# ScalarE's small copies and gate exponentials two turns further on, in the expert stage of a decoder layer

## The reference

```python
logits = jnp.einsum('btd,ed->bte', x, gate_w)
_, idx = jax.lax.top_k(logits + lb_bias, K)               # K = 2 of E = 8
w = jax.nn.sigmoid(sel_logits); w = w / (w.sum(-1) + 1e-6)
hidden = jnp.square(jax.nn.relu(jnp.einsum('nd,ehd->neh', xf, w1)))
expert_out = jnp.einsum('neh,edh->ned', hidden, w2)
moe_out = jnp.einsum('ned,ne->nd', expert_out, we)        # we: weight of each token and expert, mostly 0
shared = jnp.square(jax.nn.relu(x @ cfc.T)) @ cproj.T
```

## Time and profile before

| | us |
|---|---|
| median of 3 runs | 491.29 (489.8 to 491.65) |
| profiled execution | 488.51 |
| its span in the trace | 486.7 |
| PE busy in the span | 440.3 (90%) |
| DVE busy | 333.7 (69%) |
| ACT busy | 265.6 (55%) |
| POOL busy | 162.1 (33%) |
| expert stage, first up to last residual add | 409.5 to 484.0 |

### The profile page before, as it was taken

The page is one execution under the profiler, slowest core; times in us unless marked ns, Lnnn a source line. Parts: engine busy times, 40 slices in busy tenths (PEclk is TensorE's granted clock), DMA queues, the critical chain, the costliest instruction groups (busy, mean ns, idle before and its releaser), DMA issues.

```text
span 486.7 us, 17235 instructions
## 1 busy us (share of the span) xinstructions
PE 440.3 (90%) x7304; PEld 276.1 (57%) x7304; DVE 333.7 (69%) x668; ACT 265.6 (55%) x811; POOL 162.1 (33%) x95
## 2 busy tenths in 40 slices
PE   0778999999999799999799999998888989999996
PEld 0444655665755555655575675574445435666765
DVE  5555787666977667886847987867677596565633
ACT  2545646666466456555535655545544456554653
POOL 7148384332350963350851432093300000001000
PEclk9999999999999899999889999999989899999999
DMA  8221000000000000000000000000000004404150
GB/s 286 70 73 48 20 9 23 26 18 9 27 25 1 24 18 11 25 24 2 24 4 24 2 5 1 3 4 2 1 1 1 1 1 174 175 23 162 35 195 24
DMA packets 17465, 19.49 MB, mean 40 GB/s; under 512 B 1659, under 2 KB 14575, under 8 KB 17263
## 3 DMA queue, kind: packets, MB, share of 16 engines
q1 hardware_dynamic: 17391, 18.41, 11.2%
HBM read 16.17 MB, written 2.16 MB: 38 GB/s over the span
## 4 chain that ended last, share of the span: by engine, by line
PE 67%; DVE 18%; issue 5%; ACT 5%; DMA 3%; POOL 1%; SPq 0%; DVEq 0%; ACTq 0%; POOLq 0%
PE psT L1489 15%; PE psS L1460 13%; PE psS L1470 8%; PE psOM L1426 7%; PE psT L1859 5%; PE psS L1842 4%; DVE neg_max L1086 2%; DVE x_max L1069 2%; ACT prob L692 2%; PE psOM L1570 2%; PE psS L1689 2%; DMA q_both<-w_scratch 2%; PE psT L1570 2%; DVE pt_even L1050 2%; PE psOM L1716 1%
## 5 line engine op out<-in xcount | busy, mean ns | idle before, releaser
L692 ACT ACTIVATE prob<-psS,neg_max 128x208 f32<-128x208 f32 (+23 forms) x256 | 120.9, 479 | 71.2 <-DVE neg_max L1086 40.1
L475 POOL TENSOR_TENSOR stat<-stat,pack_a_sb 128x4 f32<-128x4 f32 (+2 forms) x16 | 54.7, 3417 | 163.3 <-DVE stat L912 116.9
L1086 DVE TENSOR_REDUCE neg_max<-psS 128x2 f32<-128x672 f32 (+9 forms) x96 | 77.0, 802 | 43.1 <-PE psS L1470 42.3
L1489 PE MATMUL psT<-pack_a_sb,prob 128*128 128x128 f32 (+4 forms) x640 | 95.9, 285 | 6.6 <-DVE pt_even L1050 3.5
L1489 PEld LDWEIGHTS psT<-pack_a_sb,prob 128*128 128x128 f32 (+4 forms) x640 | 65.7, 133 | 45.8 <-issue 27.0
L1460 PE MATMUL psS<-k_v,q_both 64*32 64x336 f32 (+23 forms) x2048 | 88.8, 402 | 3.0 <-ACT prob L692 1.7
L1470 PE MATMUL psS<-rel_shifted,q_both 36*32 36x268 f32 (+16 forms) x2048 | 72.4, 339 | 0.0
L509 POOL TENSOR_TENSOR q_both<-qT,pack_a_sb 128x1024 f32<-128x1024 f32 x16 | 31.7, 1981 | 84.3 <-PE psS L1470 81.9
L1470 PEld LDWEIGHTS psS<-rel_shifted,q_both 36*32 36x32 f32 x2048 | 37.9, 109 | 24.5 <-issue 17.5
L692 ACT ACTIVATION_READ_ACCUMULATOR prob<-psS,neg_max 128x1 f32 x256 | 50.9, 199 | 0.0
L1859 PEld LDWEIGHTS psT<-pack_b_sb,prob 128*128 128x128 f32 x288 | 36.1, 191 | 18.3 <-DVE prob L1332 11.1
(11 more groups left out here) (173 smaller groups left out, 606.7 us busy)
## 6 DMA issues: line engine op xcount, KB each, us to landing
q_rep<-q_scratch SPq DMA_DIRECT2D x128, 32.0 KB
k_v<-w_scratch SPq DMA_DIRECT2D x8, 512.0 KB, 6.6
q_both<-w_scratch SPq DMA_DIRECT2D x8, 512.0 KB, 6.6
pack_b_sb<-pack_b_dram SPq DMA_DIRECT2D x1, 1641.5 KB, 9.7
X<-x_dram SPq DMA_DIRECT2D x4, 256.0 KB, 5.3
q_scratch<-qT SPq DMA_DIRECT2D x4, 256.0 KB, 2.0
out_dram<-X SPq DMA_DIRECT2D x4, 256.0 KB, 2.3
pack_a_sb<-pack_a_dram SPq DMA_DIRECT2D x1, 535.0 KB, 4.4
```

The lines of the kernel that those rows point to most:

```text
L475: nc.gpsimd.tensor_tensor(st[:, 5, 0:groups], st[:, 2, 0:groups], ca["root"][0:parts, 0:groups], ALU.pow).then_inc(seeded, 1)
L692: ins = nc.scalar.activation(prob[:, s % 4, half, 0:wide], psS[:, bank + half, at:at + wide], ACT.Exp, bias=neg_max[:, s % 4, half:half + ...
L1086: v.tensor_reduce(neg_max[:, s % 4], psS[:, bank:bank + 2, 0:read_width(*divmod(s, BS))], AX_X, ALU.max, negate=True).then_inc(max_ready, 1)
L1489: ins = nc.tensor.transpose(psT[0:w, k % 2, at:at + T], prob[:, s % 4, half, j * T:j * T + w], ident)
```

## The change

In the expert stage, each of ScalarE's eight small instructions stands two turns further on: behind square(k+2) where it stood behind square(k). What they compute, and the orders of TensorE, VectorE, GpSimd and SyncE, stay.

```diff
-                if b == 0 and i == 1:
+                if b == 0 and i == 3:
                     copy_weights(1, psO[0:TB * E, 0:T])
-                if b == 0 and i == 3:
+                if b == 0 and i == 5:
                     copy_back(B - 1)
-                if b == 0 and i == 4:
+                if b == 0 and i == 6:
                     copy_front(2, psO[:])
-                if b == 0 and i == 6:
+                if b == 0 and i == 8:
                     exp_gate(2, psO[:, 0:TB * E])
-                if b == 1 and i == 4:
+                if b == 1 and i == 6:
                     copy_weights(2, psM[0:TB * E, T:2 * T])
-                if b == 1 and i == 8:
+                if b == 2 and i == 1:
                     copy_front(3, psO[:])
-                if b == 2 and i == 0:
+                if b == 2 and i == 2:
                     exp_gate(3, psM[:, 0:TB * E])
-                if b == 2 and i == 6:
+                if b == 2 and i == 8:
                     copy_weights(3, psM[0:TB * E, T:2 * T])
```

## The result

| | before | after |
|---|---|---|
| median of 11 runs each (us) | 490.22 | 487.82 |
| ratio of the runs, 95% interval | | 0.9943 (0.9923 to 0.9964) |
| profiled execution | 488.51 | 487.04 |
| first up in its trace | 409.52 | 411.24 |
| expert stage, first up to the end of the last residual add | 74.45 | 71.27 |

The account below looks back on a forecast made before the run. PE, busy 90% of the span, was taken as the bound, with eight downs late behind DVE and ACT. Removed 4.21 less 0.6 added gives 3.6 us: 491.29 to 487.7 us, range 486.0 to 490.5 (8 in 10).

Parts of the forecast that it names:

- seven late downs: Downs of turns 2, 4, 7, 14, 16, 19 and 25, late before; forecast to give back 4.21 us in all.
- The rule by which a late down costs its printed idle time plus 0.27 us: PE in the expert stage: the loss per late down is about printed idle plus 0.27; 5.18 us over eight downs.
- Turn 2: Late down(2): weigh(2), freed from square(2), starts about 0.55 earlier, first weight load still not hidden; 0.55 of 0.67 us goes.
- Turn 16: Late down(16), at the end of a layer-norm chain begun after the late weigh(14): its whole 0.71 us goes.
- turn 10: Late down(10), which hangs on DVE's routing arithmetic behind e_add(0): stays late at 0.85 us.
- The tight places: Readers of moved results; tightest is gate(3) waiting for copy_front(3), 0.35 us to spare: costs nothing, at worst 0.3.
- the load behind copy_weights(3): Load that weigh(28) needs lands late, so down(28) stalls anew: 0.5 to 1.1 us, taken as 0.6.
- U + 2.1: U is the start of the up in PE's turn k; ACT reaches the moved small instruction 2.1 us later.
- The page on transfers: Advice against the change, borne out at weigh(28) alone; taken alone, the change would cost 0.6 us there and nothing else.
- Half comes back: Rival, chance 0.19: turn 16 stays late, copy_front(3) misses by 0.3, first load takes 4.4 or more; 2.1 us gained, 489.2.
- The stalls did not change their name: Rival, chance 0.10: DVE's own order would hold the weighs back instead of ACT; 0 to 1 us goes, 491 us.
- ACT kept its lead: Rival "slower", chance 0.06: square(k) comes in turn k-1 instead of k-2, each turn loses 0.4; 494.5 us for 17 turns.

Follow-up runs that it names:

- e1: Kernel before with only copy_weights(1), copy_back, copy_front(2) and exp_gate(2) moved two turns on: expert stage 72.75 us, against 74.45 before.
- e2: Kernel before with only copy_weights(2), copy_front(3) and exp_gate(3) moved two turns on: expert stage 72.49 us.
- e4: Kernel before with all the moves but that of copy_weights(3): expert stage 70.79 us.
- e10: As e9, with DVE's routing arithmetic of sequence 2 moved behind weigh(10), (11) and (12) in three parts: ratio 0.9899, median 485.05 us, stage 69.29 us.
- e7: Changed kernel with copy_weights(3) three turns on instead of two, behind square(27): expert stage 72.49 us.
- e9: Changed kernel with copy_weights(3) and the PE transpose that feeds it one turn earlier: ratio 0.9912, median 485.85 us, stage 70.14 us.
- e3: Kernel before with only copy_weights(3) moved two turns on: expert stage 75.54 us.
- e8: Changed kernel with 110 already fulfilled waits added at the start of PE's stream: expert stage 71.13 us.
- e5: Changed kernel with copy_weights(3) one turn on instead of two, behind square(25): expert stage 71.54 us.
- e6: Kernel before with all eight small instructions moved one turn on instead of two: expert stage 71.66 us.

## Why the prediction was right, and where it was off

**The bound and the mechanism held.** The forecast said that ACT waited its lead of two turns away in front of eight small instructions, and that each of seven late downs hung on that. e1, e2 and e4 took the parts asunder and met 72.7, 72.5 and 70.8 with 72.75, 72.49 and 70.79. The rule by which a late down costs its printed idle time plus 0.27 us gave every sum to 0.03.

**The number was partly luck.** 487.7 stands 0.1 beside the measured 487.82, but the forecast took 3.6 off 491.29, and over eleven runs the kernel before takes 490.22. What can be compared is the gain: 3.6 forecast, 2.8 timed (1.8 to 3.8), 3.18 in the stage.

**Turn 2** was put at 0.55, with the first weight load still exposed. It gave the whole 0.67: down(2) follows its up in 0.86 (417.97 to 418.83) and the next up 0.89 later. DVE started weigh(2) 0.41 behind its last step on the cross-attention, which was just early enough.

**Turn 16** went with turn 14, as forecast, and **turn 10** stayed at 0.85; e10 shows that it was DVE's order alone.

**The tight places.** Gate(3), which had 0.35 us to spare for copy_front(3), started 0.86 behind its up (450.06 to 450.92): no wait. Nor did any other reader of a moved copy or exponential hold PE.

**The step that was mis-sized is the load behind copy_weights(3)**: 0.6 us in the sum, 1.14 in the trace, just above the 0.5 to 1.1 that it was given (and 0.86 printed, where I had said 0.3 to 0.8). Its upper end stood for a slower load, which did not come. The start of the copy (U + 2.1) and the first load (3.8) were right; "issued 1.69 after the copy" was not, since the store took 2.1 us to land instead of 1.4. I had gone through SP's own orders, but not through what else uses the DMA engines. In the trace of before no packet of instructions lay beside the four stores, and nothing in it priced that. With 4.33 - 0.6 the gain would have been 3.7. All of the difference between 3.6 and 3.18 is this, less the 0.12 of turn 2.

**The page on transfers** (the Trainium skill, "DMA: Bandwidth & Descriptors", section "Rules for kernel authors": issue early, wait late) was worth the weight that it got, and more: in e7 the copy is one turn later and down(28) costs 2.36 us instead of 1.14, and in e9 it is a turn earlier and down(28) costs nothing.

**The rivals.** "Half comes back" priced the late load at 1.1 to 1.2, and 1.14 came, but from the store's landing and not from a load of 4.4; its other two conditions, turn 16 and copy_front(3), did not come true. The stalls did not change their name, and ACT kept its lead: in most turns it waited 0.64 us for up.

**Still open**: why the packets of PE's instructions moved. In the changed kernel the last two of the three in the stage come at 32.1 and 52.5 us from its start, before at 38.5 and 60.0; with e3 alone only the second moved by more than a microsecond (to 56.3). The other traces sort the same way. The second of the two packets begins 2.3 to 2.8 us after up(27) in the eight that move copy_weights(3), and 6.1 to 7.0 us after it in the four that don't (e8 apart). The first begins 31.7 to 33.7 us into the stage where copy_weights(2) was moved, and at 36.8 to 38.5 where it was not. That fits a PE whose instruction stream runs further ahead once no down makes it wait, and it would explain why removing a wait put the packet on the store. No run measured how far ahead the stream is.

## What to carry to other kernels

When one in-order engine feeds a pipeline several turns ahead and also serves small requests, place each request behind the work that the engine can do until its input arrives; one turn of cover was enough here, and each turn more only makes the reader of the result later. Follow the result of each moved instruction through its transfers to the first reader, and count the cover in turns: seven late downs gave back 0.5 to 0.8 us each, and the last move, which freed one of them (0.65), made another late by 1.14. Where that cover is short, move the producer as well (e9) rather than trade one stall for another.

## What the runs showed of the hardware that was not expected

- Instructions are fetched through the same 16 DMA engines as data. One packet of 16 KB held an engine for 1.1 us in the changed kernel's trace (0.9 to 1.5 beside the 17 stores). A sixteenth of the store of 16 KB stood behind it (e5), so the store landed in 1.9 to 3.1 us where it met a packet, against 1.4 otherwise.
- The meeting belongs to the program at these two stores: it came again with the same one (2.1, then 1.9 us for sequence 3; 2.4, then 2.3 for sequence 2), and 110 waits added at the start of PE's stream, where its first product came 0.14 us later for them, took it away. It can differ between executions too. At the store of sequence 0, ahead of the stage and of all the edits but those waits, a packet lay beside it in e3, e6 and e10 (401.7 to 402.2 us, store 2.4 to 2.5); in the other traces none did, and it took 1.4.
- A store issued 0.9 us earlier in the turn landed only 0.2 us earlier when it met the packet (e5).
